# Causal attention heads: relative scores skewed by longer lines, and two matmuls with zero weights in each step

## What is computed

```
q, k, v = heads of x @ w.T                       # 2 batches x 16 heads, 16 wide
q, k = rotary(q), rotary(k);  q = q / sqrt(16)
rel = rel_emb[clip(pos_k - pos_q, -32, 32) + 32]
scores = q.k + q.rel ;  scores = where(causal, scores, -1e18)
attn = softmax(scores)
ctx  = attn @ v + attn.rel
out  = ctx @ w_o.T
```

## Time and profile before

| | |
|---|---|
| median of 3 runs | 5097.98 us |
| profiled execution, its own time | 5106.48 us |
| its span | 5104.8 us |
| granted TensorE clock, mean | 0.888 of 2.4 GHz |
| TensorE busy | 4455.2 us (87%) |
| VectorE busy | 2996.9 us (59%) |
| ScalarE busy | 2297.0 us (45%) |
| GpSimd busy | 648.1 us (13%) |
| transfers | 343.08 MB in 316682 packets, mean 67 GB/s |

### The profile page before, as it was taken

The page is one execution under the profiler, slowest core; times in us unless marked ns, Lnnn a source line. Parts: engine busy times, 40 slices in busy tenths (PEclk is TensorE's granted clock), DMA queues, the critical chain, the costliest instruction groups (busy, mean ns, idle before and its releaser), DMA issues. The chain is left out here.

```text
span 5104.8 us, 80050 instructions
## 1 busy us (share of the span) xinstructions
PE 4455.2 (87%) x25680; PEld 2625.2 (51%) x25680; DVE 2996.9 (59%) x5384; ACT 2297.0 (45%) x4375; POOL 648.1 (13%) x666
## 2 busy tenths in 40 slices
PE   7999859999999999889998965688978978889488
PEld 6888723333333333258886544345545545555355
DVE  6655668888888888456664355444444544444342
ACT  3222327777777777612222222334434434445222
POOL 2322100000000000013332024111111111111000
PEclk9999969999999999889999987778778878789699
DMA  2000311111111111039000026444444444341801
GB/s 77 0 0 1 138 50 42 42 39 41 37 37 42 42 38 33 11 113 296 0 0 18 0 86 183 112 93 93 103 95 95 105 94 96 97 98 44 133 26 33
DMA packets 316682, 343.08 MB, mean 67 GB/s; under 512 B 161280, under 2 KB 266760, under 8 KB 302600
## 3 DMA queue, kind: packets, MB, share of 16 engines
q1 hardware_dynamic: 299912, 296.20, 22.1%
q0 software_dynamic: 16384, 41.96, 2.9%
HBM read 239.26 MB, written 148.11 MB: 76 GB/s over the span
## 5 line engine op out<-in xcount | busy, mean ns | idle before, releaser
L1322 DVE TENSOR_REDUCE full_tops<-psum 128x1 f32<-128x1024 f32 x1024 | 1207.2, 1220 | 247.8 <-PE psum L1226 247.4
L1279 ACT ACTIVATE full_probs<-psum 128x512 f32<-128x512 f32 x2048 | 1067.2, 602 | 338.5 <-PE psum L1198 306.4
L1736 ACT ACTIVATE causal_probs<-psum 128x512 f32<-128x512 f32 (+3 forms) x1280 | 644.3, 533 | 761.2 <-PE psum L1622 389.4
L1784 DVE TENSOR_REDUCE causal_tops<-psum 128x1 f32<-128x1024 f32 (+7 forms) x704 | 587.4, 859 | 261.5 <-PE psum L1659 261.5
L1198 PE MATMUL psum<-full_q,full_k 49*128 49x512 f32 x2048 | 657.8, 482 | 49.5 <-ACT full_probs L1279 33.3
L1608 PE MATMUL psum<-causal_q,causal_k 49*128 49x512 f32 (+3 forms) x1280 | 465.3, 508 | 181.2 <-DMA causal_q<-causal_rows 171.0
L1198 PEld LDWEIGHTS psum<-full_q,full_k 49*128 49x128 f32 x2048 | 290.1, 189 | 640.4 <-ACT full_probs L1279 585.4
L1207 PE MATMUL psum<-full_probs,full_vh 128*32 128x512 f32 x4096 | 565.3, 625 | 0.7 <-ACT full_probs L1279 0.7
L1226 PE MATMUL psum<-full_k,full_q 48*128 48x512 f32 x2048 | 408.9, 463 | 64.7 <-DMA full_k<-qk_split 38.3
L1659 PE MATMUL psum<-causal_k,causal_q 48*128 48x512 f32 (+4 forms) x1152 | 375.2, 468 | 88.9 <-DMA causal_k<-rot_parts 46.9
L1638 PE MATMUL psum<-causal_probs,causal_vh 128*32 128x384 f32 (+3 forms) x3712 | 409.1, 501 | 1.2 <-ACT causal_probs L1736 1.2
(11 more groups left out here) (189 smaller groups left out, 6095.6 us busy)
## 6 DMA issues: line engine op xcount, KB each, us to landing
bias_tiles<-in_bias SPq DMA_DIRECT2D x4, 10240.0 KB, 86.5
causal_bias<-bias_tiles SPq DMA_DIRECT2D x32, 1280.0 KB, 27.7
band_scores<-xn POOLq DMA_DIRECT2D x192, 160.0 KB, 6.1
qk_split<-qkvf_parts SPq DMA_DIRECT2D x32, 512.0 KB, 3.4
full_q<-qk_split SPq DMA_DIRECT2D x64, 256.0 KB
full_k<-qk_split SPq DMA_DIRECT2D x64, 256.0 KB
rot_parts<-qkvc_parts SPq DMA_DIRECT2D x32, 512.0 KB, 3.1
causal_q<-rot_parts SPq DMA_DIRECT2D x64, 256.0 KB
```

The costliest lines, as they stand in the source:

```text
L1279: nc.scalar.activation(pT[:, kt % 4, n * BLK:(n + 1) * BLK], k.psum[:, bank(q, u), :], ACT.Exp).then_inc(p_ready, 1)
L1322: nc.vector.reduce_max(mx[:, q % 2, u // 2, u % 2:u % 2 + 1], src, AX_X).then_inc(m_free, 1)
L1736: nc.scalar.activation(dst, k.psum[:, bank(q, u), 0:(hi - lo) * P], ACT.Exp).then_inc(p_ready, 1)
L1784: last = nc.vector.reduce_max(mx[:, r, t, entry:entry + 1], both[:, off:off + hi - lo], AX_X)
```

## The change

In the causal heads:

- `fill_bias_tiles` is gone. A line is now one partition's row of all 16 bands and one element more (`BIAS_ROW` = 16 x 160 + 1). For each head SyncE loads the 32 values per row and tile into `compact` (`load_rel`), VectorE copies them into a half line whose mask was written once (`spread`, two halves of eight tiles, both in the one buffer `skew_rows`), SyncE stores each half as 128 lines of 5 KB (`skew(i, 0)`, `skew(i, 1)`), and the bias load reads 128 lines of 10 KB at a pitch one element shorter.
- SyncE's order in a head is `load(i+3)` and the bias load, `skew(i+4, 0)`, `store(i-1)`, `skew(i+4, 1)`, `load_rel(i+5)`, `row_load(i+1)`. VectorE does `spread(i+4, 0)` and `spread(i+4, 1)` after units 3 and 9 of its 24.
- The stores of a head go from eight to four, of 17 rows each, into one tensor `OD`; the output buffer is single instead of double.
- Band tiles use 8 places in turn instead of 16.
- In the steps after the first, TensorE does `keep_warm`: two matmuls with zero weights that add nothing to bank 7.
- ScalarE's row copy comes before the exps of units 3 and 4 of its step.

In the projections, `project_full_stage` loads the reciprocals spread by the transfer, as the other one does, and its four matmul pieces go; `project_causal_stage` reads from `OD`, its numerators in two transfers per block.

```diff
+                def load_rel(i):
+                    if not isinstance(i, int) or i > 0:
+                        sp.wait_ge(spread_done, 2 * i)
+                    sp.dma_start(compact[:, :, :], k.TD[bass.ds(i, 1), :, :, :].rearrange("a p t j -> p (a t) j")).then_inc(rel_loaded, 16)
+
+                def skew(i, part):
+                    sp.wait_ge(spread_done, 2 * i + part + 1)
+                    lines = k.BB[1:1 + NH * P * BIAS_ROW].rearrange("(h p x) -> h p x", h=NH, p=P)
+                    dst = lines[bass.ds(i, 1), :, part * HALF_ROW:(part + 1) * HALF_ROW + part].rearrange("a p x -> (a p) x")
+                    sp.dma_start(dst, skew_rows[:, 0:HALF_ROW + part]).then_inc(skewed, 16)
+
+                def load_bias(i, q):
+                    heads = k.BB[0:NH * P * BIAS_ROW].rearrange("(h x) -> h x", h=NH)
+                    src = heads[bass.ds(i, 1), 0:P * KT * BAND].rearrange("a (r t c) -> (a r) t c", r=P, c=BAND)
+                    sp.dma_start(bt[:, q, :, :], src).then_inc(bt_loaded[q], 16)
...
+                def body(i, q, left):
+                    if left > 2:
+                        sp.wait_ge(skewed, 32 * (i + 4))
+                        sp.wait_ge(pv_done, (i + 3) * NSTEP + NSTEP)
+                        load(i + 3, (q + 3) % 4)
+                        load_bias(i + 3, (q + 3) % 4)
+                    if left > 3:
+                        skew(i + 4, 0)
+                    store(i - 1)
+                    if left > 3:
+                        skew(i + 4, 1)
+                    if left > 4:
+                        load_rel(i + 5)
+                    if left:
+                        row_load(i + 1, (q + 1) % 4)
...
+                def keep_warm():
+                    for side in range(2):
+                        nc.tensor.matmul(k.psum[:, 7, 2 * side * P:2 * (side + 1) * P], zeros.bitcast(BF16), k.ident[:, :].bitcast(BF16),
+                                         start=False, stop=False, skip_group_check=True)
...
                         for ahead, h, p in maxima[:2]:
                             far(i + ahead, h, p)
+                        if n > 0:
+                            keep_warm()
...
                     for n in range(NSTEP):
-                        exps(i, q, n, (3, 4))
                         if left and n == ROW_STEP + 1:
                             act.wait_ge(row_loaded[(q + 3) % 4], 32 * ((i + 3) // 4 + (q + 3) % 4 // 3))
                             row(i + 1, (q + 1) % 4)
+                        exps(i, q, n, (3, 4))
...
+                def spread(i, part):
+                    if part == 0:
+                        dve.wait_ge(rel_loaded, 16 * (i + 1))
+                    if not isinstance(i, int) or i + part > 0:
+                        dve.wait_ge(skewed, 16 * (2 * i + part))
+                    nc.vector.memset(skew_rows[:, HALF_ROW:HALF_ROW + 1], 0.0)
+                    wide = skew_rows[:, 0:HALF_ROW].rearrange("p (t c) -> p t c", c=BAND)
+                    tiles = slice(part * KT // 2, (part + 1) * KT // 2)
+                    nc.vector.tensor_copy(wide[:, :, 0:REL], compact[:, tiles, :]).then_inc(spread_done, 1)
...
+                    more = not isinstance(i, int) or i + 4 < NH
+                    for at, (ahead, h, p) in enumerate(segment(q, left)):
...
                         far(i + ahead, h, p)
+                        if at in (2, 8) and more:
+                            spread(i + 4, at // 8)
```

```diff
-                    nc.tensor.matmul(k.psum[:, c, :], spread[0:HC, :], rd[0:HC, half, c, :],
-                                     start=True, stop=True).then_inc(rb_ready, 1)
...
+                for c in range(C):
+                    every = src[c * HC:(c + 1) * HC, :].unsqueeze(1).to_broadcast([HC, DH, BLK])
+                    sp.dma_start(rd[:, half, c, :], every).then_inc(s_ld[half], 16)
```

More of the change, by code:

```diff
@@ L1447, in heads_causal_stage @@
         o_free = sem("o_free")
-        o_stored = [sem(f"o_stored{r}") for r in range(2)]
+        o_stored = sem("o_stored")
         mm_stored = [sem(f"mm_stored{r}") for r in range(2)]
@@ L1484, in _, with load @@
             def _(sp):
[L1485 to L1492, removed]
+                def load_rel(i):
[11 more added lines that the diff above has]
+                    sp.dma_start(bt[:, q, :, :], src).then_inc(bt_loaded[q], 16)
+                def load(i, q):
                     head_rows = lambda part, x: k.QC[x][part, :, bass.ds(i, 1), :, :]
@@ L1529, in _ @@
                 sp.wait_ge(ones, 4)
-                for q in range(3):
-                    load(q, q)
+                load(0, 0)
+                skew(0, 0)
+                skew(0, 1)
+                load_rel(1)
+                load(1, 1)
+                sp.wait_ge(skewed, 32)
+                sp.wait_ge(edge_set, 16)
+                load_bias(0, 0)
+                skew(1, 0)
+                skew(1, 1)
+                load_rel(2)
+                load(2, 2)
+                sp.wait_ge(skewed, 64)
@@ L1532, in _ @@
+                load_bias(1, 1)
+                skew(2, 0)
+                skew(2, 1)
+                load_rel(3)
+                sp.wait_ge(skewed, 96)
+                load_bias(2, 2)
                 row_load(0, 0)
                 load(3, 3)
-                row_load(1, 1)
-                def body(i, q):
-                    load(i + 3, (q + 3) % 4)
-                    store(i - 1, (q + 1) % 2)
-                    row_load(i + 1, (q + 1) % 4)
+                skew(3, 0)
+                skew(3, 1)
@@ L1552, in _ @@
-                store(NH - 1, (NH - 1) % 2)
+                        body(it * 4 + q, q % 4, 5)
+                for i in range(NH - 7, NH):
+                    body(i, i % 4, NH - 1 - i)
+                store(NH - 1)
+                sp.wait_ge(o_stored, 16 * QB * (NH + 1))
                 for r in range(2):
-                    sp.wait_ge(o_stored[r], 16 * (1 + 2 * QB * NH // 2))
                     sp.wait_ge(mm_stored[r], 16 * (1 + NH // 2))
@@ L1817, in _ @@
                         far(1, 1, p)
+                spread(3, 1)
                 def body(i, q, left):
-                    for ahead, h, p in segment(q, left):
+                    more = not isinstance(i, int) or i + 4 < NH
+                    for at, (ahead, h, p) in enumerate(segment(q, left)):
                         if p == 1 and ahead == 2:
@@ L1867, in project_full_stage @@
     bias = take(D)
-    spread = take(P)
     s_w, s_rec, s_rc = sem("weights"), sem("recip_dma"), sem("recip")
     s_ld = [sem(f"loaded{r}") for r in range(2)]
-    rb_ready = sem("rb_ready")
     o_ready = sem("o_ready")
```

133 lines of the change are left out of this document (67 added, 66 removed).

## The result

The changed kernel takes 5411.18 us (median of four, 5395.24 to 5416.15) against 5097.97 for the kernel before: a ratio of 1.0603, 95% interval 1.0573 to 1.0633. The forecast was 5485, in a range of 5190 to 5650.

What follows compares the result with a forecast made beforehand. Causal heads 1 to 27 were taken as bound by transfers queued behind q and k loads on few DMA engines. 5106.5 + 331 (heads) + 60 (start) - 3 (rest) = 5494.5, less 8.5, rounded to 5485; range 5190 to 5650.

Steps and rivals of the forecast that it cites:

- A: Rival for heads 1 to 27: the skew isn't held, VectorE never stands, period taken as 44, 4984 us; chance 0.11.
- D: Rival: as A, but the queueing of the row of maxima holds the period at 48, 5098 us; chance 0.05.
- C: Rival for heads 1 to 27: clock stays low for the rest of the head, period 67.8, 5689 us; chance 0.08.
- B: Rival for heads 1 to 27: shorter wait, landing T0+28, low clock 3 us, period 51.3, 5223 us; chance 0.14.
- T0: Time mark in each causal head: head i-1's last values are done and load(i+3) starts.
- the term for calm: Landing of skew(i+4, 0): 2.2 us off the bias load's T0+34.1 for fewer bias pieces and a calmer burst; bounds 0 and 4.
- The 1.6 on top of it: Landing of skew(i+4, 0): 1.6 us added for eight lines of 5 KB on the slowest engine.
- 26.8: Heads 1 to 27: us from the landing of skew(i+4, 0) to the next T0.
- my 6.5: Heads 1 to 27: us lost per head to low clock after TensorE's wait; bounds 3 and 13.
- my 18.7: TensorE's work behind the landing at full clock: 17.7 us for steps, 1.0 for the zero matmuls.
- "fifth": Low-clock term: share of the 8.1 us loss credited to the zero matmuls, leaving 6.5.
- The stores: SyncE's four 17-row stores a head instead of eight issues: 0 us, being behind the landing that decides; felt only in A.

Runs made afterwards that it cites:

- e1: Changed kernel with skew(i+4, 0) issued ahead of the eight q and k loads instead of behind them: 5347.77 us, ratio 1.0466 to the kernel before.
- e2: Changed kernel with VectorE's second copy, spread(i+4, 1), moved from after unit 9 to after unit 21: 5204.26 us, ratio 1.0185 to the kernel before.
- e3: Changed kernel with the eight q and k loads split into 24 of 8 rows each, same bytes: 5233.8 us, ratio 1.0274 to the kernel before.
- e5: e1 with each 17-row store cut into one of 16 rows and one of a single row: 5189.56 us, ratio 1.016 to the kernel before.

## Why the prediction was right, point by point

**The mechanism** was the one forecast: `skew(i+4, 0)` is queued behind the loads, `spread(i+4, 1)` waits for it, the maxima stand behind that copy and TensorE behind the maxima. Its signs are there: VectorE idle once a head after the third step (17.6 us on the mean, some 20 forecast), TensorE 15.1 on the mean and 16.8 at the most (17 to 21 forecast, too much), no more waits for the row but one, part 0 landing at 24.1 and part 1 at 6.5, a clock of 0.76 (near 0.7 forecast), and 37 a head from head 28 on (36 forecast). e1, e2 and e3 each took away one link and the wait shrank. A and D fall with the first row of waits. C falls with the clock, which is back at 1.00 by 3426. B's landing of T0+28 is missed by 3.4 us, the forecast's by 2.1; its period of 51.3 is the further off.

**The size.** The forecast was 388 us on the span, and 306.1 came:

| | forecast | measured | from |
|---|---|---|---|
| heads 1 to 27 | +331 | +249 | 27 x 57.29 for 27 x 48.07, by SyncE's T0 |
| start, T0 of head 1 | +60 | +36 | 3321.88 for 3285.84 |
| heads 28 to 31 | 0 | +4 | 148 for 144 |
| full projection | -8 | 0 | 76.9 for 77.3 |
| causal projection | +5 | +12 | 150.05 for 138.02 |
| fill of the bias tiles | 0 | 0 | TensorE 509.7 of 520, before 512.1 |
| elsewhere | 0 | +5 | the rest |

*Heads 1 to 27* were 3.0 us a head too dear. 2.1 of it is the landing, T0+31.4 for T0+33.5, and there the term for calm was the one mis-sized. I took 2.2 off the old landing of the bias load, T0+34.1. In the changed kernel the bias load is issued at T0+6.6 and lands 23.3 us later (27.7 before), at T0+29.9: 4.2 sooner. The 1.6 on top of it for the store was right, for the store is down 1.5 later. The other 0.9 lies behind the landing: 25.9 measured for 26.8. The copy and TensorE's restart take 0.9 for 1.6. The low clock takes 12.4 us on the mean, which by the step times of the earlier trace rows costs 12.4 x (1 - 4.25/7.44) = 5.3 for my 6.5. What is left, 19.7, is work at full clock and is longer than my 18.7: two terms too large and one too small. The 6.5 came near as a mean of very unlike heads (3.3 to 30.4 us of low clock), and the "fifth" in it had no row behind it. The zero matmuls start 0.23 us ahead of what follows, for my 0.24.

Three places of the written sum don't come out of their own terms, and none changes the forecast. The bounds of the landing are T0+29.7 and T0+37.6 by their terms, not 30 and 37, with nothing to spare. Steps 4 to 7 are 4 x 4.25 = 17.0, not 17.2. The range is said to leave out only the top of C, but C's 5689 lies outside it.

*The start*, step by step: first skew down at 3172 (forecast 3174), the copy behind the first bias at 3204 (3209), `skew(2, 0)` at 3241 (3256), `skew(3, 0)` at 3281 (3306), and from there 41 us to the second T0 (40), at 3321.88. SyncE's queue there, each row a part 0 and the wait for the copy of part 1 behind it:

```profile
3152.10 20.53 SPq L1491 DMA_DIRECT2D bias_tiles<-causal_skew_rows  x2
...
3215.43 26.25 SPq L1491 DMA_DIRECT2D bias_tiles<-causal_skew_rows  x2
...
3257.97 22.86 SPq L1491 DMA_DIRECT2D bias_tiles<-causal_skew_rows  x2
```

The two rounds of load and skew in the middle took 37 and 39 us where I had 47 and 50.

*The projections* were both mis-sized within their bounds. The full one lost its four pieces and gained nothing. TensorE's busy time in it falls from 52.5 to 39.0 us, but its waits for VectorE's multiplication (L2002, L1941 before) rise from 6.9 to 40.7 in eight. One is of 26.3 us at the start, where it had waited 20.6 for the reciprocals; the others are of some 2.06 for 0.86. So TensorE's own pieces were not what bounded a block. Of the causal one's +12 the waits for the band loads make 11 (102.6 us for 91.6). Whether the second transfer of the numerators lengthens them was not tested.

*That the total misses by just the 82 us of the heads is luck.* The 24 us by which the start came in too dear are balanced by 4, 8, 7 and 5 elsewhere, which I had at less or at nothing.

*The stores* at 0 stood in the changed kernel, but only because the late landing made the row late too. The sentence that named them as dangerous in rival A was the one that mattered as soon as the landing was repaired. The rule of the Trainium skill named there ("DMA: Bandwidth & Descriptors", the section cited above) puts 17 rows on one engine. e1 against e5 is in line with it: cut to 16 and 1, the same bytes go out in 8 to 10 us for 25 to 27. No row shows on how many engines the stores ran.

## What to carry to other kernels

A wait for a transfer is set by what stands ahead of it in its queue: before adding one, look up how late a like transfer from the same place lands (here 27.7 us), and put the wait either behind that time or the transfer ahead of the large loads (e2 and e1; neither alone gave back all of the loss). On one in-order queue nothing urgent may stand behind an instruction that waits for a late producer, which made the difference of 5078 to 4877 here by moving one transfer in the order. And when one wait is repaired, ask which of the costs that it covered comes next: here the stores, then the row behind the loads, then the row behind the late copy.

## What the runs showed of the hardware that was not expected

- Four stores of 17 rows hold the issuing SyncE for 23 to 26 us in the changed kernel and 25 to 27 in e1 behind the eight loads, 11 to 22 in e3 behind the 24, and 4.1 to 4.3 with no loads ahead. Eight stores of 16 and 1 rows hold it for 8 to 10 behind the eight loads (e5).
- 24 loads of 8 rows are issued in 9.9 us, some 0.36 us each (six in 2.13 in e3), where eight with the same bytes take 0.63 to 0.77 each in the head shown of the changed kernel; three times the count costs the skew 3.3 us at the issue and brings it 9.3 at the landing.
- The row's transfers land in 1.9 to 4.3 us in e1 and in 1.8 to 15.5 in e5, with only the number of rows in the stores changed and so the time at which the row is handed over.
- Two zero matmuls a step raise the granted clock by 0.02 to 0.03 in a kernel that waits (0.73 to 0.76) and in one that doesn't (0.92 to 0.94), and change the time in neither by what can be measured.
